# Cross attention on one core: values and sums of two chunks in one odd slot, and a new order of the division, the residual row and the split contexts in even slots

## The reference

```python
Q, K, V = split_heads(x @ Wq + bq), split_heads(ctx @ Wk + bk), split_heads(ctx @ Wv + bv)
attn = softmax(einsum('bhqd,bhkd->bhqk', Q, K) / sqrt(32))
out = merge_heads(einsum('bhqk,bhkd->bhqd', attn, V)) @ Wo + bo + x
result = (out - mean(out)) * rsqrt(var(out) + 1e-5) * gamma + beta
```

## Time and profile before

| | |
|---|---|
| median of 3 runs | 623.29 us (622.09 to 623.36) |
| profiled execution | 622.21 us, span 620.4 us |
| TensorE clock granted, mean | 0.995 of full |
| busy share of the span | PE 96%, DVE 80%, ACT 58%, POOL 72% |
| ScalarE's wait for p_q ahead of qh, list of waits, 100 to 560 us | 85.6 us in 56 |
| one cl on GpSimd (L1069), page | 1299 ns |
| accumulator read behind y (L880), VectorE | 0.08 us |
| chain that ended last | PE 87%, DVE 3%, ACT 1% |

### The profile page before, as it was taken

One profiled execution on the slowest core, in us unless ns is written; L12 is line 12 of the kernel. 1 busy time (PEld: TensorE's weight loads), 2 busy tenths in 40 slices (PEclk: granted clock), 3 DMA queues, 4 the chain that ended last, 5 costly groups with the idle time before them and its releaser, 6 DMA issues.

```text
span 620.4 us, 12034 instructions
## 1 busy us (share of the span) xinstructions
PE 594.8 (96%) x3336; PEld 430.5 (69%) x3336; DVE 496.9 (80%) x913; ACT 362.9 (58%) x674; POOL 443.7 (72%) x395
## 2 busy tenths in 40 slices
PE   5998999999999999999999999999999999999992
PEld 5986765677777777777777777777777777777562
DVE  5423468888888888888888888888888888898776
ACT  5621235566666666666666666666666666655562
POOL 1335024648888888888888888888888888888785
PEclk9999999999999999999999999999999999999997
DMA  8859878988979898989898987979897989796523
GB/s 306 308 224 185 205 181 224 206 189 193 235 192 232 212 215 214 224 203 219 201 229 205 221 226 193 235 201 227 207 219 205 211 218 231 196 221 168 168 76 128
DMA packets 93392, 129.58 MB, mean 209 GB/s; under 512 B 49936, under 2 KB 49936, under 8 KB 93360
## 3 DMA queue, kind: packets, MB, share of 16 engines
q1 hardware_dynamic: 74352, 94.42, 60.8%
q10 hardware_dynamic: 19008, 34.78, 21.8%
HBM read 53.94 MB, written 24.35 MB: 126 GB/s over the span
## 4 chain that ended last, share of the span: by engine, by line
PE 87%; DVE 3%; issue 1%; ACT 1%; DVEq 0%; ACTq 0%
PE p_q L586 29%; PE p_o L652 27%; PE p_s L616 10%; PE p_v L627 10%; PE p_a L602 6%; PE p_o L99 3%; DVE nm L933 1%; PE p_a L669 1%; PE p_den L635 1%; DVE rden L898 0%; PE p_q L669 0%; ACT prob L721 0%; DVE part L888 0%; PE p_s L669 0%; ACT qh L736 0%
## 5 line engine op out<-in xcount | busy, mean ns | idle before, releaser
L721 ACT ACTIVATE prob<-p_s 77x512 f32<-77x512 f32 x256 | 143.2, 591 | 103.3 <-PE p_s L616 93.0
L1069 POOL TENSOR_TENSOR cl<-cxt,ch 128x512 fp32r<-128x512 f32 x64 | 83.1, 1299 | 110.0 <-ACT ch L746 110.0
L933 DVE TENSOR_REDUCE nm<-p_a 128x4 f32<-128x308 f32 x256 | 115.9, 475 | 49.1 <-PE p_a L602 48.0
L888 DVE TRANSPOSE_TENSOR_REDUCE part<-prob 96x64 f32<-96x2048 f32 x64 | 146.4, 2287 | 1.6 <-issue 1.3
L736 ACT ACTIVATE qh<-p_q,bq_col 128x512 fp32r<-128x512 f32 x64 | 44.0, 687 | 124.6 <-PE p_q L586 124.6
L586 PE MATMUL p_q<-xh,wqh 128*128 128x512 f32 x256 | 101.1, 395 | 1.7 <-PEq L151 1.7
L586 PE MATMUL p_q<-xl,wqh 128*128 128x512 f32 x256 | 101.2, 395 | 0.0
L586 PE MATMUL p_q<-xh,wql 128*128 128x512 f32 x256 | 101.0, 394 | 0.0
L616 PE MATMUL p_s<-z,ks 97*77 97x512 f32 x256 | 95.6, 413 | 2.4 <-ACT prob L721 2.4
L652 PE MATMUL p_o<-woh,ch 128*128 128x512 f32 x240 | 95.4, 398 | 0.8 <-issue 0.7
L652 PE MATMUL p_o<-wol,ch 128*128 128x512 f32 x240 | 94.6, 394 | 0.0
(11 more groups left out here) (128 smaller groups left out, 930.1 us busy)
## 6 DMA issues: line engine op xcount, KB each, us to landing
z<-qh SPq DMA_DIRECT2D x256, 128.0 KB, 3.8
z<-ql SPq DMA_DIRECT2D x124, 128.0 KB, 4.8
xn<-in_x ACTq DMA_DIRECT2D x60, 256.0 KB, 3.3
out_dram<-y SPq DMA_DIRECT2D x60, 256.0 KB, 4.3
xt<-in_x_t ACTq DMA_DIRECT2D x58, 256.0 KB, 5.0
ks<-k_high SPq DMA_DIRECT2D x32, 154.0 KB, 4.8
cx<-in_ctx_t SPq DMA_DIRECT2D x4, 616.0 KB, 6.0
k_high<-kth SPq DMA_DIRECT2D x4, 616.0 KB, 3.6
```

The costliest lines, as they stand in the source:

```text
L721: nc.scalar.activation(prob[0:S2, j, :], p_s[j % 2][0:S2, :], ACT.Exp, scale=SCALE).then_inc(prob_ready, 1)
L888: nc.vector.tensor_reduce(part[:], prob[0:KP, :, :].rearrange("p h (i r) -> p (h i) r", r=DK), AX_X, ALU.add, apply_transpose=True).then_i ...
L933: nc.vector.tensor_reduce(nm[:, t, g.k % 2:HALF:2], p_a[t % 2][:, 0:HC * S2].rearrange("p (h k) -> p h k", k=S2), AX_X, ALU.max, negate=Tr ...
L1069: nc.gpsimd.tensor_tensor(cl[:, i, g.k % NCH, :], cx[:, g.k % 2, :], ch[:, i, g.k % NCH, :].bitcast(F32), ALU.subtract).then_inc(cl_ready, 1)
```

## The change

- From two slots' `values` and `sums` one group is made, `values_of_pair`, in odd slots: values of chunks g-5 and g-4, each into a bank of its own (p_v0, p_v1), and then the sums of both in four pairs of matmuls of 32 columns instead of 16. The sums lie in unused columns of the first p_a bank, since p_den has become the second p_v. Even slots have neither. prob, part and rec get two buffers. Chunks 60 to 63 (`single`) go as before.
- The first p_a of an odd slot waits for the reciprocal of the sums. `project_out` waits for ch and cl chunk by chunk instead of for all four.
- VectorE, even slots: `add_residual` first, then `spread` and `divide` of chunk g-5 (the odd chunk of the last pair), `q_low`, row maxima 0 and 1, `sum_keys` of chunk g-4, row maxima 2 and 3. Odd slots: `sum_keys`, `add_residual`, `q_low`, one reciprocal for both chunks, `spread` and `divide` of the even chunk, row maxima.
- ScalarE: in even slots `ctx_high` of chunk g-5 is first, ahead of `q_high`; in odd slots it stands behind the exponentials. Variance and minus mean over standard deviation move from VectorE to ScalarE, as one and two short instructions, in slots up to 63.
- GpSimd: in even slots it begins with `ctx_low` of chunks g-6 and g-5; in odd slots it has none.
- Two small constants and a smaller scratch for DMAs that GpSimd would issue (it issues none here).

```diff
+            def values_of_pair(g):
+
+                at_least(pe, cx_ready, g.over(1, -1))
+                values(g.back(1))
+                values(g)
+                pe.wait_ge(part_ready, g.over(1, 1))
+                at_least(pe, rec_ready, g.over(1, -1))
+                at_least(pe, max_ready, g.over(1, LAG_PV, QT) - 1)
+                for j in range(HC):
+                    last = nc.tensor.matmul(den_pair[DK * j:DK * (j + 1), :].rearrange("p (i r) -> p i r", r=QB), sel[:],
+                                            part[:, :, QB * j:QB * (j + 1)], start=True, stop=True)
+                last.then_inc(pv_summed, 2)
...
-                if v.valid(NG) and g.valid(NG):
-                    values(v)
-                    sums(v)
+                if v.valid(NG) and g.valid(NG) and g.k % 2 == 1:
+                    values_of_pair(v)
...
+                if t == 0 and g.k % 2 == 1 and g.back(LAG_PV).valid(NG):
+                    pe.wait_ge(rec_ready, g.back(LAG_PV).over(1, 1))
...
 ScalarE, slot(g)
+                w = v.back(1)
+                if g.k % 2 == 0 and w.valid(NG) and not single(w):
+                    ctx_high(w)
                 if g.valid(NG):
                     q_high(g)
...
 VectorE, slot(g)
+                w = v.back(1)
+                if m.valid(NS) and g.valid(NG) and g.k % 2 == 0:
+                    add_residual(m)
+                if g.k % 2 == 0 and w.valid(NG) and not single(w):
+                    spread(w)
+                    divide(w)
-                if v.valid(NG):
+                if v.valid(NG) and (g.k % 2 == 1 or not g.valid(NG)):
                     sum_keys(v)
...
                 if g.valid(NG):
                     q_low(g)
...
+                if v.valid(NG) and not single(v) and g.k % 2 == 1:
+                    invert_sums(v)
+                    spread(w)
+                    divide(w)
...
                         row_maxima(g, t)
+                        if t == 1 and v.valid(NG) and g.k % 2 == 0:
+                            sum_keys(v)
...
 GpSimd, slot(g)
+                w, e = v.back(1), v.back(2)
+                if g.k % 2 == 0 and e.valid(NG) and not single(e):
+                    ctx_low(e)
+                if g.k % 2 == 0 and w.valid(NG) and not single(w):
+                    ctx_low(w)
```

More of the change, by code:

```diff
@@ L274, in _ @@
                 nc.gpsimd.memset(keep["minus_half"][:], -0.5)
+                nc.gpsimd.memset(keep["eps"][:], EPS).then_inc(keep["eps_set"], 1)
                 sel = keep["sel"]
@@ L363, in attend @@
         nm, nmt = sb("nm", [P, QT, DK], F32), sb("nmt", [P, 2, QT, DK], F32)
-        prob = sb("prob", [P, HC, S], F32)
-        part = sb("part", [KP, HC * QB], F32)
-        rec = sb("rec", [P, QB], F32)
+        prob = sb("prob", [P, 2, HC, S], F32)
+        part = sb("part", [KP, 2, HC * QB], F32)
+        rec = sb("rec", [P, 2, QB], F32)
         rden = sb("rden", [P, S], F32)
@@ L373, in attend @@
         ve, rstd, nmr = (sb(n, [P, 4, 1], F32) for n in ("ve", "rstd", "nmr"))
-        ysum, ssd, nmean = (sb(n, [P, 4, 1], F32) for n in ("ysum", "ssd", "nmean"))
-        p_q, p_v, p_den, p_o = (psum(n) for n in ("p_q", "p_v", "p_den", "p_o"))
+        ysum, ssd, nmean, over_d = (sb(n, [P, 4, 1], F32) for n in ("ysum", "ssd", "nmean", "over_d"))
+        p_q, p_o = (psum(n) for n in ("p_q", "p_o"))
+        p_v = [psum(f"p_v{i}") for i in range(2)]
         p_s = [psum(f"p_s{i}") for i in range(2)]
@@ L412, in attend @@
                       (p_s[0], prob_ready, NG * HC)]
-        gamma_tail, beta_tail = p_s[1], p_den
+        gamma_tail, beta_tail = p_s[1], p_v[1]
         x_last = [xt[:, 0, :], xt[:, 1, :], bv_row[:], vb[:, B % 2, :]]
@@ L434, in last_tile, with single, pair_end @@
             return None
+        den_pair = p_a[0][:, HC * S2:HC * S2 + 2 * QB]
+        den_single = p_v[1][:, 0:QB]
+        def single(v):
+            return isinstance(v.u, int) and PAIR * v.u + v.k >= NG - LAG_PV
+        def pair_end(v):
+            return v.over(1, 1) if single(v) else Slot(v.u, v.k | 1).over(1, 1)
         def is_last(c):
@@ L623, in values @@
                     pe.wait_ge(vb_in[g.k // NCH % 2], g.over(PAIR, 1, 16))
-                at_least(pe, cx_ready, g.over(1))
+                bank = p_v[0] if single(g) else p_v[g.k % 2]
                 for j in range(HC):
                     h = HC * (g.k % NCH) + j
-                    nc.tensor.matmul(p_v[DK * j:DK * (j + 1), :], vb[0:S2, g.k // NCH % 2, DK * h:DK * (h + 1)],
-                                     prob[0:S2, j, :], start=True, stop=True)
+                    nc.tensor.matmul(bank[DK * j:DK * (j + 1), :], vb[0:S2, g.k // NCH % 2, DK * h:DK * (h + 1)],
+                                     prob[0:S2, g.k % 2, j, :], start=True, stop=True)
+            def values_of_pair(g):
[9 more added lines that the diff above has]
+                last.then_inc(pv_summed, 2)
             def sums(g):
@@ L634, in sums @@
                 for j in range(HC):
-                    last = nc.tensor.matmul(p_den[DK * j:DK * (j + 1), 0:QB], sel[:], part[:, QB * j:QB * (j + 1)],
+                    last = nc.tensor.matmul(den_single[DK * j:DK * (j + 1), :], sel[:], part[:, g.k % 2, QB * j:QB * (j + 1)],
                                             start=True, stop=True)
@@ L646, in project_out @@
                         pe.wait_ge(wo_low, KC)
[L647 to L649 removed]
                     at_least(pe, y_ready, m.over(1))
+                if t == 0:
+                    pe.wait_ge(ch_ready, m.over(QT, 0, KC) + kc + 1)
+                    pe.wait_ge(cl_ready, m.over(QT, 0, KC) + kc + 1)
                 for n, (x, w) in enumerate(((ch, woh), (ch, wol), (cl, woh))):
@@ L693, in slot @@
                 if not g.valid(NG):
+                    pe.wait_ge(cx_ready, v.over(1))
                     values(v)
@@ L718, in exp @@
                         act.wait_ge(const_pool, 2)
-                    at_least(act, pv_summed, g.over(1))
-                    at_least(act, part_ready, g.over(1))
-                nc.scalar.activation(prob[0:S2, j, :], p_s[j % 2][0:S2, :], ACT.Exp, scale=SCALE).then_inc(prob_ready, 1)
+                    at_least(act, pv_summed, pair_end(g.back(2)))
+                    at_least(act, part_ready, g.over(1, -1))
+                nc.scalar.activation(prob[0:S2, g.k % 2, j, :], p_s[j % 2][0:S2, :], ACT.Exp, scale=SCALE).then_inc(prob_ready, 1)
             def split_x_high(n):
@@ L753, in square, with variance, mean_over_std @@
                                      accum_out=ssd[:, i, :]).then_inc(squared, 1)
+            def variance(m):
+                i = m.k % 4
+                act.wait_ge(squared, m.over(1, 1))
+                nc.scalar.activation(ve[:, i, :], ssd[:, i, :], ACT.Identity, bias=keep["eps"][:],
+                                     scale=1.0 / D ** 3).then_inc(ve_ready, 1)
+            def mean_over_std(m):
+                i = m.k % 4
+                act.wait_ge(rstd_ready, m.over(1, 1))
+                nc.scalar.mul(over_d[:, i, :], rstd[:, i, :], -1.0 / D).then_inc(over_d_ready, 1)
+                act.wait_ge(over_d_ready, m.over(1, 1))
+                nc.scalar.activation(nmr[:, i, :], ysum[:, i, :], ACT.Copy, scale=over_d[:, i, :]).then_inc(nmr_ready, 1)
             def load_residual(m):
@@ L804, in slot @@
                     square(m)
+                    if g.valid(NG):
+                        variance(m)
                 if g.back(LAG_NORM - 2).valid(NS):
@@ L809, in slot @@
                     exp(s, 3)
-                if v.valid(NG):
+                if g.k % 2 == 1 and w.valid(NG) and not single(w):
+                    ctx_high(w)
+                if v.valid(NG) and single(v):
                     ctx_high(v)
+                if g.back(LAG_NORMALIZE).valid(NS) and g.valid(NG):
+                    mean_over_std(g.back(LAG_NORMALIZE))
                 if g.back(LAG_NORMALIZE).valid(NS):
@@ L886, in sum_keys @@
                 dve.wait_ge(prob_ready, g.over(1, 1, HC))
-                at_least(dve, pv_summed, g.over(1))
-                nc.vector.tensor_reduce(part[:], prob[0:KP, :, :].rearrange("p h (i r) -> p (h i) r", r=DK),
+                at_least(dve, pv_summed, pair_end(g.back(2)))
+                nc.vector.tensor_reduce(part[:, g.k % 2, :], prob[0:KP, g.k % 2, :, :].rearrange("p h (i r) -> p (h i) r", r=DK),
                                         AX_X, ALU.add, apply_transpose=True).then_inc(part_ready, 1)
@@ L917, in divide @@
                 at_least(dve, cl_ready, g.over(1, -1))
-                nc.vector.tensor_tensor(cx[:, i, :], p_v[:], rden[:], ALU.mult).then_inc(cx_ready, 1)
+                nc.vector.tensor_tensor(cx[:, g.k % 2, :], p_v[0 if single(g) else g.k % 2][:], rden[:], ALU.mult).then_inc(cx_ready, 1)
             def q_low(g):
@@ L963, in slot @@
                     q_low(g)
-                if v.valid(NG):
+                if v.valid(NG) and single(v):
                     invert_sums(v)
```

(7 more changed lines are left out.)

35 lines of the change are left out of this document (22 added, 13 removed).

## The result

The changed kernel takes 634.5 us (633.9 to 636.2) against 623.3 us before: the ratio is 1.019, with a 95% interval of 1.0165 to 1.021. It is slower, as forecast (629.7, range 614.5 to 636.5), by 11.2 us where 6.4 were forecast (629.7 was added up from the profiled 622.2 us; its terms make 7.5). Its profiled execution took 633.9 us with a span of 631.8, and the rest of this text reads that one.

The account below looks back on a forecast made before the run. TensorE, busy 66.20 of 66.20 us over eight steady slots, was taken to bound the kernel. From the profiled time, 622.2 - 8.4 + 12.3 + 2.0 + 1.6 = 629.7 us, range 614.5 to 636.5.

Parts of the forecast that it names:

- What goes from TensorE: Slots 8 to 63: values, sums and first scores cost 0.30 us less a pair, -8.4 us over 28 pairs.
- The best case of the bounds: TensorE's saving per pair of slots at its upper bound, with the sums no dearer: 0.34 us.
- The chain onto qh: Even slots: VectorE and ScalarE work ahead of qh makes the first p_a 0.44 us late, +12.3 us over 28 pairs.
- The ten steps: From the odd slot's last p_a to the even slot's first p_a, through VectorE and ScalarE: sum 4.54 us.
- The loop: First even slot of each of five loop passes: turn to next instruction .63 instead of .24 us, +2.0 us.
- Behind slot 63: Slot 64: rden and division of chunk 59 delay the values of chunk 60 and so the sums, +1.6 us.
- GpSimd's cl: Both cl in even slots end before the p_o groups that need them in every fourth slot: hidden by .8 us.
- the short operations: Variance and minus mean over std on ScalarE, at most 1.8 us a slot, hidden behind exponentials: 0.
- What was called hidden: Moved work on VectorE, ScalarE, GpSimd and DMAs up to slot 63 that was forecast to cost TensorE 0.
- sum_keys between the row maxima: Even slot, VectorE: 2.23 us between second and third row maxima; the odd chunk's sum_keys result still hidden by .5.
- the reciprocal ahead of the odd slot's first p_a: Odd slot: reciprocal done at O+5.5, first p_a due at O+6.0, hidden by .5 us.
- the covered chain: Rival: several of the ten steps onto qh overlap, the wait is 0, time 615.4 us; chance 0.24.

Follow-up runs that it names:

- The version with neither wait nor loop: Changed kernel with qh ahead of ch in even slots, values of chunk 60 not waiting for chunk 59's division, all slots written out: 618.0 us, ratio .9912.
- their control run: Kernel before with variance and minus mean over standard deviation moved from VectorE to ScalarE: 624.0 us, ratio 1.0008.
- cl of 59 later: The version with qh ahead of ch and earlier values of chunk 60, with GpSimd's cl of chunk 59 behind the bias row in slot 64: 622.1 us.
- the first try: The version with qh ahead of ch, with values of chunk 60 in slot 64 not waiting for chunk 59's division: 619.1 us.
- the two last versions: The version with qh ahead of ch, earlier values and cl of chunk 59 later: with the loop 622.1 us, with all slots written out 620.1 us.

## Why the prediction was right, and where its sizes were off

It named the right mechanism, place and sign; the size was 11.4 us in the profiled executions where its terms make 7.5. Term by term, over slots 8 to 63:

- **What goes from TensorE.** Forecast -8.4 us, 0.30 a pair. The version with neither wait nor loop has 456.6 against 464.9: -8.3. The second set of values is .86 (1.85 less .99), the first scores of the even slot .46, as taken; the sums were .06, not .08. (The best case of the bounds adds up to .33, not .34.)
- **The chain onto qh.** Forecast +12.3, 0.44 a pair. After with no loop against the version with neither: 467.8 - 456.6 = 11.2, 0.40 a pair, and 0.42 in the slot shown. The ten steps, taken from six different stretches of the trace of before, came out as .34 and .52, .23, .59, .74, .69, .03, .53, .68 and .16: a sum of 4.51 for 4.54.
- **The loop.** Forecast +2.0 us, measured 5.8: the term that was most mis-sized. I had read one gap, turn to the next instruction in the first slot of a pass (.63 for .24 in the earlier trace rows). The chain crosses several such gaps, and each now counts: .47 there, .16 between rden and cxt, .17 between qh and p_a, and 0.1 to 0.2 in every other even slot of a pass. One of them could be read in the trace of before: rden to cxt took .90 in its slot 32 too, where it was hidden.
- **Behind slot 63.** Forecast +1.6, measured +2.8. The wait of the values was right: forecast 2.08 us behind the start of the residual row, measured 2.07 (585.38 to 587.45). The sums came 4.2 us behind the start of the values and not 2.4, for TensorE was at the lower clock from about 588 to 591. But that isn't what the rest was paid for. The changed kernel without a loop stood the same 2.39 us, kept a clock of 1.00, had its sums 2.6 us behind the start of the values as forecast, and took 47.2 us there all the same. What both have, and the forecast left out, is the residual row of slot 65: it starts 10.4 us behind slot 63's last p_a (7.3 before), behind ch of chunk 59 and GpSimd's cl, scale, shift and bias row. Up to 1.0 us of the 2.8 may belong to the short operations (their control run). Of the changed kernel without a loop:

```profile
580.99 1.06 PE L635 MATMUL p_v<-prob,vb 77*32 77x512 f32 x8 [2.39 <-DVE cxt L974]
...
583.58 0.26 PE L656 MATMUL p_v<-part,sel 96*32 96x16 f32 x8
```

```profile
588.21 0.69 DVE L926 SCALAR_TENSOR_TENSOR y<-p_o,xn 128x512 f32<-128x512 f32 x1 [2.52 <-POOL xn L1146]
```

- **What was called hidden was hidden** up to slot 63: the short operations (TensorE at 66.20 of 66.20 in their control run), sum_keys between the row maxima, the reciprocal ahead of the odd slot's first p_a (at + 6.01, as due), GpSimd's cl (none waited for by p_o in the steady slots), z's DMAs. The forecast had odd slots at 9.2 and even ones at 7.5; they are 9.17 and 7.49 outside the loop.

Of the rivals, the covered chain was false, and the version with qh ahead of ch shows what it would have been: 619.2 measured, 615.4 worked out; 2.6 of the difference are the same two terms, the loop (1.4 left in first slots of a pass) and the drain (1.2). The rule of the Trainium skill that the next Vector instruction starts when the pipe of the last is empty ("VectorE: DVE Perf Modes", "The DRAIN you can't avoid") would have put the residual row's step at .76; it took .59 on the chain itself. The .3 us per ACTIVATE that the Trainium skill gives in "ScalarE: Activation LUTs", "Rules for kernel authors", agrees with what the trace now shows for one element a row where the bias or the scale is an operand, .29 to .30 us; with neither it took .20.

## What to carry to other kernels

When work moves to another slot, write the chain from the last instruction that feeds it to the first that needs it, through all engines in their program order, and compare it with the bound engine's own work over the same stretch; here 4.51 us against 4.10 decided a change whose saving was real. One instruction placed ahead of another that is due earlier costs its wait as well as its time: of the same change, qh ahead of ch makes a gain of 0.6% out of a loss of 1.9%. And a loop of five passes cost 0.5 us in the kernel before and 1.6 with qh ahead of ch, where TensorE's own queue was the bound, but 5.8 us where a chain hopped between engines.

## What was not expected of the hardware

The runs of one and the same kernel (cl of 59 later) differed by up to 5.1 us along with the mean granted clock: 617.7 us at 0.994 and 622.8 at 0.982. In the drain the clock fell to its lower level behind stands of TensorE of 1.2 to 2.4 us, and stayed there while the engine was busy again: for some 3.4 us in the changed kernel, with qh ahead of ch and in the first try, 6.8 us in the first try without a loop, and some 10 us in the two last versions. It is not the stand alone: the changed kernel without a loop stood the same 2.39 us in slot 64 and its clock stayed at 1.00. Short stands of 0.4 us in every even slot, in the changed kernel, left it at 1.00.
